# Weighting products of 32 columns instead of 18, and V copies and first transpose later in the order, in a window-attention and convolution kernel

## What is computed

```python
def L0(x, ac_w, ac_b, qkv_w, proj_w, proj_b):      # 16 heads of 8, windows of 8 x 8 pixels
    g = clip((x * ac_w + ac_b) * x, 0.0, 6.0)
    q, k, v = split_into_windows_and_heads(einsum('bchw,dc->bdhw', g, qkv_w))
    attn = softmax(einsum('wnqd,wnkd->wnqk', q, k) * 8 ** -0.5)
    o = einsum('wnqk,wnkd->wnqd', attn, v)
    return einsum('bchw,dc->bdhw', back_to_image(o), proj_w) + proj_b
x = x + L0(group_norm(x), ...)
x = x + conv3x3(group_norm(x), W) + bias            # 128 -> 128 channels, padding 1
```

## Time and profile before

| | us |
|---|---|
| runs | 1821.16, 1818.70, 1819.74 |
| median of the runs | 1819.74 |
| the profiled execution, its own time | 1822.06 |
| its span (first to last instruction) | 1820.3 |
| TensorE (PE) busy | 1474.0 |
| VectorE (DVE) busy | 991.4 |
| ScalarE (ACT) busy | 772.1 |
| GpSimd (POOL) busy | 376.5 |

### The profile page before, as it was taken

The page is one execution under the profiler, slowest core; times in us unless marked ns, Lnnn a source line. Parts: engine busy times, 40 slices in busy tenths (PEclk is TensorE's granted clock), DMA queues, the critical chain, the costliest instruction groups (busy, mean ns, idle before and its releaser), DMA issues. The chain is left out here.

```text
span 1820.3 us, 53510 instructions
## 1 busy us (share of the span) xinstructions
PE 1474.0 (81%) x21475; PEld 930.1 (51%) x21475; DVE 991.4 (54%) x1379; ACT 772.1 (42%) x1039; POOL 376.5 (21%) x243
## 2 busy tenths in 40 slices
PE   1598888888898888597846998988898988977876
PEld 0266655556566666332324665665665666653332
DVE  7444434434444443499974444444444444418998
ACT  1344434434444443354423444444444444434443
POOL 3101111111111110256530111111111111004656
PEclk9996656555555655599975555565555565558999
DMA  5454435444444542022336544454444454400111
GB/s 203 129 128 121 128 98 127 108 108 107 108 116 119 128 119 73 1 69 99 109 112 160 122 111 113 122 125 114 111 113 111 123 127 116 108 19 13 58 46 69
DMA packets 169169, 190.78 MB, mean 105 GB/s; under 512 B 30208, under 2 KB 145280, under 8 KB 167936
## 3 DMA queue, kind: packets, MB, share of 16 engines
q1 hardware_dynamic: 168960, 187.58, 38.8%
HBM read 118.29 MB, written 67.11 MB: 102 GB/s over the span
## 5 line engine op out<-in xcount | busy, mean ns | idle before, releaser
L671 DVE TENSOR_REDUCE m_all<-ps 128x16 f32<-128x1024 f32 x256 | 312.2, 1220 | 371.8 <-PE ps L876 371.8
L910 PE MATMUL ps<-v_ext,work 128*64 128x18 f32 x8192 | 446.9, 262 | 60.2 <-ACT work L462 60.1
L910 PEld LDWEIGHTS ps<-v_ext,work 128*64 128x64 f32 x8192 | 419.1, 207 | 108.9 <-ACT work L462 72.2
L462 ACT ACTIVATE work<-ps,ws 128x1024 f32<-128x1024 f32 x256 | 284.4, 1111 | 303.7 <-PE ps L892 302.2
L382 POOL TENSOR_TENSOR g_lo<-work,g_hi 128x512 f16<-128x512 f32 x64 | 73.8, 1153 | 1145.8 <-ACT g_hi L507 1145.8
L838 PE MATMUL ps<-work,c_hi 128*128 128x512 f16 x384 | 151.2, 394 | 68.3 <-DVE work L758 68.2
L876 PE MATMUL ps<-k_bd,q_pl 48*64 48x128 f16 x4096 | 151.3, 289 | 18.4 <-DMA q_pl<-stack_scratch 11.1
L876 PEld LDWEIGHTS ps<-k_bd,q_pl 48*64 48x64 f16 x4096 | 94.5, 144 | 136.9 <-issue 133.5
L698 DVE BATCH_NORM_STATS2 st<-img (+1 forms) x64 | 44.4, 693 | 212.4 <-POOL img L387 212.4
L758 DVE TENSOR_TENSOR work<-work 128x640 f16<-128x640 f32 x128 | 152.5, 1195 | 5.7 <-ACT work L546 5.5
L546 ACT CAST work<-work 128x640 f16<-128x640 f32 x128 | 91.8, 719 | 145.5 <-DVE work L754 98.2
(11 more groups left out here) (122 smaller groups left out, 1939.7 us busy)
## 6 DMA issues: line engine op xcount, KB each, us to landing
stack_scratch<-work SPq DMA_DIRECT2D x128, 256.0 KB, 2.0
k_bd<-stack_scratch SPq DMA_DIRECT2D x256, 96.0 KB
q_pl<-stack_scratch SPq DMA_DIRECT2D x128, 192.0 KB, 3.7
q_bd<-stack_scratch SPq DMA_DIRECT2D x256, 96.0 KB
k_pl<-stack_scratch SPq DMA_DIRECT2D x128, 192.0 KB, 5.2
stack_scratch<-work SPq DMA_DIRECT2D x128, 128.0 KB, 2.0
out_dram<-work SPq DMA_DIRECT2D x32, 512.0 KB, 2.7
img<-in_x_dram SPq DMA_DIRECT2D x8, 1024.0 KB, 12.7
```

The lines of the kernel that those rows point to most:

```text
L462: a.activation(probs[:, p % 2, :], ps[:, ST_B:ST_B + 2, :].rearrange("p w t -> p (w t)"), ACT.Exp, scale=ws[:, R_EXP:R_EXP + 1]).then_inc( ...
L671: v.tensor_reduce(m_all[:, 0, :, p], ps[:, S_B:S_B + 2, :].rearrange("p r (a k) -> p (r a) k", k=WIN), AX.X, ALU.max).then_inc(max_done, 1)
L910: mm = t_.matmul(ps[64 * w:64 * w + 64, PV_B + p // 2, col:col + VC], probs[:, p % 2, at:at + WIN], v_ext[:, md % BUFS, 2 * p + w, hp, :], ...
```

## The change

`VC` becomes 4 * 8 = 32: `v_ext` grows to 32 columns for each pair of heads, of which the last 14 stay zero, and each weighting product moves 32 columns and writes 32. The division reads the same 18 at the wider stride. Four lines follow from that. On ScalarE the copy to `g_hi` and the affine step now stand ahead of the V copies, and these stand directly ahead of the exponential of round 0. On PE `turn(n - 1, 0)` moves behind `scores(3)` and `weigh(n, m, 0)`.

```diff
-VC = 2 * HD + 2
+VC = 4 * HD
...
-            g.memset(ve[64:P, :, 2 * HD + 1:VC], 1.0).then_inc(pool_set, 1)
+            g.memset(ve[64:P, :, 2 * HD + 1:2 * HD + 2], 1.0).then_inc(pool_set, 1)
...
                     if "E" in on:
                         exps(n - 1, 3)
+                    if "H" in on:
+                        after(act, g32_done, n + 3)
+                        after(act, v_done, n)
+                        if peeled(i, -2) and b:
+                            after(act, cadd_done, b * CUNITS - 1)
+                        a.copy(g_hi[:, m % BUFS, :], g32).then_inc(g_hi_done, 1)
+                    if "G" in on:
+                        row, col = pixels(i + 4)
+                        if peeled(i, -4):
+                            act.wait_ge(coef_ready, 2 * b + 1)
+                            after(act, x_lo_done, b * CUNITS - 1)
+                        after(act, gpre_done, n + 3)
+                        a.activation(aff.rearrange("p (r c) -> p r c", r=WS), img[:, bass.ds(row, WS), bass.ds(col, UCOL)],
+                                     ACT.Identity, scale=cf[:, A_SLOPE:A_SLOPE + 1], bias=cf[:, A_OFF:A_OFF + 1]).then_inc(aff_done, 1)
                     if "B" in on:
...
                         for e in range(2):
                             a.copy(v_ext[64 * e:64 * e + 64, mb, :, :, HD * e:HD * e + HD].rearrange("p w h d -> p (w h) d"),
                                    v_heads(e)).then_inc(v_out, 1)
-                    if "H" in on:
...
                     if "D" in on:
                         exps(n, 0)
-                    if "G" in on:
...
                     if "D" in on:
                         exps(n, 1)
...
-                        v.reciprocal(rec[h], bank[:, :, 2 * HD:VC]).then_inc(rec_done, 1)
+                        v.reciprocal(rec[h], bank[:, :, 2 * HD:2 * HD + 2]).then_inc(rec_done, 1)
...
                         scores_t(n, m, 0)
+                    if "C" in on:
+                        scores(3)
+                    if "D" in on:
+                        weigh(n, m, 0)
                     if "E" in on:
                         if "B" in on:
                             after(pe, v_out, n + 2)
                         after(pe, ot_out, n - 2)
                         turn(n - 1, 0)
-                    if "C" in on:
-                        scores(3)
                     if "D" in on:
-                        weigh(n, m, 0)
                         scores_t(n, m, 1)
```

## The result

The change made the kernel faster: 1716.86 us median of four runs (1704.63 to 1731.59) against 1820.14 for the kernel before beside them, a ratio of 0.941 (95% interval 0.936 to 0.946). Ratios here leave out runs that lie more than 1.5% above the fastest of their kernel, here the one of 1731.59; medians are over all runs. The forecast of 1623 us had the sign, and about twice the gain (197 us against 103). The profiled execution took 1717.58 us.

A forecast was written before the change was run, and what follows sets the result against it. Attention was taken as bound by PE at the low clock. A unit of 20.5 − 0.4 (order) − 3.0 (clock) = 17.1 us saves 197 us over 58 units, giving 1623 us; range 1460 to 1800.

The forecast's parts named there:

- What bounds it: Attention stages: PE at the low clock is the bound; other engines and transfers do not come near.
- Term 1: Weighting products: the weight load covers the move of 32 columns, costing only a tail of 0.06 us a unit.
- width is not covered: Rival: moving adds to the load in weighting, 1.8 us a unit, 1900 us; chance of slower 0.10.
- Terms 2 and 3: New order on ScalarE and PE: earlier exponential and residual add, shorter PE waits; 0.4 us a unit after the tail.
- order alone: Rival: more columns do not move the clock, only the new order gains; 1797 us, chance 0.20.
- Term 4: Attention stages: denser weighting brings 4.5 us more high clock a unit, −3.0 us, clock about 0.73.
- The sign of being wrong: A unit above 20.5 us, or PE waiting for a transfer in each unit, would make the whole forecast wrong.
- Nothing moves: Rival: the unit stays at 20.5 us as the high stretch slides into PE's wait; 1820 us, chance 0.05.

The follow-up runs named there:

- act_order32: Kernel before with 32 columns and the new order on ScalarE alone, PE's order as before: median 1702.64 us, four runs from 1648.97 to 1756.12.
- wide23: Kernel before with PE's new order alone, 18 columns in weighting rounds 0 and 1 and 32 in rounds 2 and 3: 1720.64 us, 0.947.

## Why the prediction was right or wrong

- *What bounds it*, and that the clock does not follow PE's busy time: right. With the new order, the experiments that changed the columns moved while the loads stayed (24, 32, 64) all moved the clock. The Trainium skill ("TensorE: Matmul & The Clock Gate", section "What's actually happening") puts the release of the throttle down to activity, without columns. The runs show that how busy the records make PE look does not tell it: the kernel with 64 columns has PE busy for 74% of its span and a mean clock of 0.85, the kernel before 81% and 0.67.
- *Term 1, width is covered*: right. 1.83 became 1.85, and the rival "width is not covered" (1900 us) fell with it.
- *Terms 2 and 3, order*: 0.4 us a unit was forecast, 0.54 measured between low units (21.54 and 21.00). The steps went as said: wait for the residual add gone, wait ahead of L987 gone, exponential earlier. As a time of its own, "order alone, 1797 us" was 14 us too low: the low unit shrank by 0.60, but units with a high stretch gained only 0.2 to 0.3 us and more units had none.
- *Term 4, the clock*: it had the sign and half of the cause, the columns, which do little without the order; its size failed. "4.5 us high more, under halfway: −3.0" gave a unit of 17.1 us and a clock of 0.73. Measured, 28 units with 10.24 us high and 23 with none make 5.6 us a unit, 2.2 more than the 3.4 before; their mean is 18.4 us, and the clock in the attention stages is 0.63, from 0.57. The amount of high clock was the mis-sized part. The price of 0.67 for each further high us would make 1.5 us of the 2.2, and the mean came out 1.7 below the forecast's 20.1. Over a whole high stretch the worth is less, (21.00 − 16.30) / 10.24 = 0.46 us, for part of it still falls on PE's 1.98 us wait ahead of weighting 0.
- *The sign of being wrong*, "a unit above 20.5 us", did appear, in 23 units of 21.00 us. It was badly chosen: these are wholly low units, which took 21.54 before, and the kernel is faster by the 28 others.
- *What no step said*: that width and order need each other. I added a gain of the width to a gain of the order, 3.0 and 0.4 us. Alone they were worth under 1 us and 7 us in all (1818.4 less 1817.8 and 1811.0), together 103. So the two aren't a sum. That the forecast came out on the right side is in part luck: the same working, applied to the width alone, would have given 3.0 us a unit and about 1650 us, where 1817.8 was measured.
- *Nothing moves*, given 0.05, came nearest to what the width alone did: its unit stayed at 20.51 us.

What the runs don't settle: what exactly a run of work needs for the clock to rise, since the same run is followed by it in one unit and not in another; whether the wait ahead of the maxima's transpose is what width alone suffers from; why ScalarE's new order makes units alternate where PE's alone gives 17.0 us each; why act_order32 scatters by 6%; and how the width of rounds 2 and 3 helps in wide23.

## What to carry to other kernels

Where TensorE is the bound and the granted clock is at 0.50 while its busy share is near 1, look at how many columns move under each weight load: columns that the load covers are nearly free and can lift the clock. Then look where in the loop the high stretch starts, for here one of 3.4 us ahead of a wait was worth 1.0 us (21.54 to 20.51) and one of 10.2 us ahead of bound work 4.7 (21.00 to 16.30). Test the parts of such a change together as well as alone, with several runs of each, since neither part need show anything.

## What was not expected of the hardware

- A fixed program took very different times from run to run: act_order32 between 1649 and 1756 us, where width alone stayed within 0.6%. Only its fastest run has a trace. So a single profile of such a kernel does not stand for its runs.
- Less can be faster: leaving ScalarE's order as it was made a kernel with 32 columns 45 us faster than the whole change, and the same choice made one with 64 columns 72 us slower.
- Runs of equal length were followed by different clocks: from weighting 0 to weighting 1 it is 5.71 us with width alone (337.63 to 343.34) and 5.72 in the changed kernel (563.32 to 569.04), with a pair of transposes in place of 0.34 us of waiting, and the clock rose behind the second and not the first. The pair isn't what it takes, for act_order32 has neither the pair nor the wait and the clock rises there too, behind 5.10 us.
